# An eight-batch adaLN attention and FFN kernel: TensorE's fillers deepened, the FFN weight's coding spread over GpSimd and ScalarE, ScalarE's first three exponentials moved ahead

## The chip, the cores and the metric

The kernel runs on one core of one Trainium2 chip. The metric is the device time of one execution in microseconds (us), the median of three runs.

## What is computed

The input x is 8 batches of 512 tokens with 256 channels. Two blocks follow each other; the gates, scales and shifts come from a small condition vector.

```python
mod = (_silu(L0_c) @ L0_wmod).reshape(L0_c.shape[0], 6, 1, -1)
sa, ca, ga, sb, cb, gb = (mod[:, 0], ..., mod[:, 5])
h = _layernorm(x, axis=-1) * (1 + ca) + sa
x = x + ga * _L0_attn_ref(h, Wq, bq, Wk, bk, Wv, bv, Wo, bo)
h = _layernorm(x, axis=-1) * (1 + cb) + sb
x = x + gb * _L0_ffn_ref(h, weight, bias)
```

The attention has 16 heads of 16 channels and a log-sparse mask: row i attends to itself and to i - 1, i - 2, i - 4, ... i - 256 (10 offsets), while masked scores count as 0 in the softmax and not as minus infinity. The FFN is one matrix product with both operands quantised in blocks of 32 (amplitude / 7.5 as the scale, values rounded to a 6-bit grid).

## The kernel before

Five engines run programs written out by hand, and semaphores tie them together. All arithmetic is float32 but for the codes (FP8) and three-way split biases (bf16). The work of a batch is a pipeline over all engines, and the programs overlap several batches:

- **ScalarE** (`act`) gathers sums and squares of the next x (`sums_before`, `squares_before`, lines 1188 and 1197), normalises it (`norm_before`, line 1174), evacuates hT, k, v and the attention, computes the exponentials (`exps`, lines 1425 to 1438), takes x1 and its statistics (`take_x1`, `squares_after`), normalises x1 (`norm_after`, line 1174 too), and codes to FP8 (`quantised`, line 1421).
- **TensorE** (`pe`) transposes, projects q, k and v (`k_rows` 826, `q_rows` 837, `v_rows` 853), sums the products of q and shifted k over each head (`head_sums`, 937 and 951), turns the scores to one token per partition (`scores_by_token`, 963 and 966), turns the attention (`attention_transposes`, 893), and does the output projection (988) and the FFN (1067).
- **VectorE** (`dve`) makes ten q-k products per batch (line 1710 for batch 0, in two halves of ten; line 1721 later), the softmax (`softmax_max`, 1802 and 1806; `softmax_weights`, 1819 to 1827), ten products of weight and v (line 1851), and the block maxima and scalings of the quantisation.
- **GpSimd** (`pool`) adds the ten weight-v products of a batch in nine additions (`add`, line 677), gates the projection weights (626, 639), makes 1/sqrt of variances (649, 658) and modulates the second norm (`modulate`, 375 and 380).
- **SyncE** issues all loads and stores. v is written to DRAM and read back shifted by 1 to 64 rows, seven times a batch.

VectorE's loop over batches b does: softmax maximum and weights of b, then weight-v products of b interleaved with q-k products of b+1. ScalarE's iteration b starts with `exps(b)` and ends with `copy_scores(b+1)`, `seed_q(b+2)` and a norm. For iterations 0 to 4 that norm is `norm_before(b+3)`, which waits for GpSimd's 1/sqrt; `exps(b+1)` stands behind it. GpSimd's iteration b is: modulation of b-2, additions 1 to 6 of b with the weight gate between, `rstd_before` or `rstd_both` for the next norms, additions 7 to 9. A weight-v product may be at most four ahead of the additions (a ring of four buffers). SyncE's load of x(b+3) waits for the norm of b+2, as it overwrites its input.

Before the loop, the program turns the weights and works off batch 0. TensorE opens the q banks with bf16 matmuls of three rows of ones and repeats such matmuls (`keep_busy`, line 752) while it waits for the condition vector and for silu. VectorE makes the statistics of batch 0, evacuates wk and wq, seeds q with its bias, then quantises the FFN weight in six steps (`setup_ffn_weight`, lines 1696 to 1703): block maximum, scale, reciprocal, scaling, coding to FP8 by an addition of `TIE_DOWN`, and scaling back. Then come the q-k products of batch 0 (`first_qk_products`), channel half 1 first, and `setup_rows`, which makes the gates. The quantised FFN weight is turned by TensorE in iteration 1 (`weight_transposes(4)`).

## Time and profile before

| what | before |
|---|---|
| median of 3 runs | 286.92 us (286.64 to 287.34) |
| profiled execution, its own time | 286.72 us |
| its span | 285.0 us |
| VectorE busy | 258.8 us, 91% of the span |
| TensorE matmuls busy | 255.6 us, 90% |
| ScalarE busy | 212.5 us, 75% |
| GpSimd busy | 210.5 us, 74% |
| DMA queue of the kernel | 53.63 MB, 60.1% of 16 engines |

The span runs from the first to the last instruction of the profiled execution; 1.7 us of its own time lie outside it. A row of the timeline gives the start and the length of an instruction (or of several of one kind in a row, with their count), and in brackets how long its engine had stood idle before it and which instruction released it. Each float32 matmul that is not a transpose leaves two records. The starts of two rows that follow each other without a bracket are the cost of the first.

### The profile page before, as it was taken

What the parts mean: (1) busy time and instruction counts of PE and PEld (TensorE: products, weight loads), DVE (VectorE), ACT (ScalarE), POOL (GpSimd) and SP (SyncE); (2) the same over time, 40 slices, a digit from 0 to 9 for tenths busy, and PEclk for the clock granted to TensorE, in tenths of its full rate; (3) what the DMA queues carried; (4) which work ended last, traced back from release to release, by engine and by line L of the source; (5) the groups of instructions that cost most, each with busy time, mean ns of one, the idle gap of its engine ahead of it and who ended that gap; (6) DMA issues with size and microseconds to landing.
All of it is one profiled execution on the core that took longest, in us unless ns stands there. A gap on an engine that the chain in (4) does not pass through costs nothing.

```text
span 285.0 us, 4442 instructions
## 1 busy us (share of the span) xinstructions
PE 255.6 (90%) x1368; PEld 158.8 (56%) x1368; DVE 258.8 (91%) x326; ACT 212.5 (75%) x577; POOL 210.5 (74%) x152
## 2 busy tenths in 40 slices
PE   6999997697978795989999999999999988997885
PEld 1653554175526561666556646664567646794663
DVE  3699799969995999999999999999999999999970
ACT  2386987975697779879898989887776937575752
POOL 7101439895879999999999999999999699845100
PEclk9999999999999999999999999999999999999999
DMA  7743977694784239724993389347943965730005
GB/s 225 193 181 81 340 248 232 230 338 133 240 273 148 73 125 350 251 72 131 295 336 127 129 263 286 135 113 222 333 147 94 279 198 178 230 103 11 0 26 199
DMA packets 54399, 53.91 MB, mean 189 GB/s; under 512 B 4100, under 2 KB 52824, under 8 KB 54376
## 3 DMA queue, kind: packets, MB, share of 16 engines
q1 hardware_dynamic: 54376, 53.63, 60.1%
q8 instruction: 11, 0.18, 0.3%
q14 instruction: 12, 0.10, 0.1%
HBM read 44.90 MB, written 8.72 MB: 188 GB/s over the span
## 4 chain that ended last, share of the span: by engine, by line
DVE 39%; POOL 19%; PE 18%; issue 11%; ACT 11%; DVEq 0%; POOLq 0%; ACTq 0%
POOL pv_buf L677 14%; DVE prod L1721 9%; DVE pv_buf L1851 9%; DVE prod L1851 4%; DVE prod L1710 4%; PE ps L988 3%; PE ps L1067 3%; PE ps L826 2%; ACT dump L1197 2%; PE ps L853 2%; ACT dump L1238 1%; DVE ps L1825 1%; PE ps L837 1%; DVE ps L1827 1%; POOL rstd L658 1%
## 5 line engine op out<-in xcount | busy, mean ns | idle before, releaser
L677 POOL TENSOR_TENSOR pv_buf<-pv_buf 128x1024 f32<-128x1024 f32 (+2 forms) x60 | 132.5, 2209 | 15.0 <-DVE pv_buf L1851 9.8
L1721 DVE TENSOR_TENSOR prod<-ps,kT 128x1024 f32<-128x1024 f32 (+4 forms) x70 | 75.1, 1110 | 0.0
L1851 DVE TENSOR_TENSOR pv_buf<-v_shift,ps 128x1024 f32<-128x1024 f32 x49 | 59.1, 1212 | 0.0
L937 PE MATMUL ps<-prod,sel_sum 128*32 128x512 f32 x256 | 30.8, 598 | 8.5 <-DVE prod L1721 7.8
L853 PE MATMUL ps<-wT,h_cen 128*128 128x256 f32 x128 | 29.9, 379 | 0.0
L826 PE MATMUL ps<-hT,wT 128*128 128x512 f32 x64 | 29.7, 596 | 0.0
L837 PE MATMUL ps<-hT,wT 128*128 128x512 f32 x64 | 29.3, 599 | 0.0
L988 PE MATMUL ps<-wo_g,w_raw 128*128 128x256 f32 x112 | 27.9, 392 | 0.0
L853 PEld LDWEIGHTS ps<-wT,h_cen 128*128 128x128 f32 x128 | 23.9, 190 | 6.4 <-issue 3.8
L988 PEld LDWEIGHTS ps<-wo_g,w_raw 128*128 128x128 f32 x112 | 20.1, 189 | 5.4 <-issue 3.2
L937 PEld LDWEIGHTS ps<-prod,sel_sum 128*32 128x32 f32 x256 | 6.7, 109 | 28.0 <-issue 13.8
L1067 PE MATMUL ps<-wf_g,w_raw 128*128 128x256 f32 x80 | 19.7, 391 | 0.0
L1851 DVE TENSOR_TENSOR pv_buf<-v_base,ps 128x1024 f32<-128x1024 f32 (+2 forms) x21 | 19.4, 950 | 0.2
L1291 ACT ACTIVATE kT<-ps,bias_cols 128x512 f32<-128x512 f32 x16 | 10.9, 686 | 11.6 <-PE ps L826 11.6
L649 POOL TENSOR_TENSOR rstd<-var,minus_half 128x4 f32<-128x4 f32 x4 | 4.1, 1016 | 20.1 <-ACT var L1201 19.3
L1174 ACT ACTIVATE x_norm<-x_in,shift,rstd 128x256 f32<-128x256 f32 x28 | 14.5, 594 | 5.6 <-POOL shift L651 3.2
L837 PEld LDWEIGHTS ps<-hT,wT 128*128 128x128 f32 x64 | 11.7, 190 | 12.4 <-issue 12.4
L826 PEld LDWEIGHTS ps<-hT,wT 128*128 128x128 f32 x64 | 11.6, 190 | 10.5 <-issue 9.0
L1067 PEld LDWEIGHTS ps<-wf_g,w_raw 128*128 128x128 f32 x80 | 14.5, 189 | 3.6 <-issue 2.0
L1174 ACT ACTIVATE x_norm<-x,shift,rstd 128x256 f32<-128x256 f32 x28 | 14.5, 592 | 1.4 <-POOL shift L668 1.4
L380 POOL TENSOR_TENSOR h<-x_norm,rows_mod 128x1024 f32<-128x1024 f32 x6 | 14.2, 2362 | 0.5
L375 POOL TENSOR_TENSOR x_norm<-x_norm,rows_mod 128x1024 f32<-128x1024 f32 x6 | 14.2, 2364 | 0.3 <-ACT x_norm L1174 0.2
(212 smaller groups left out, 550.3 us busy)
## 6 DMA issues: line engine op xcount, KB each, us to landing
v_shift<-v_rows SPq DMA_DIRECT2D x56, 512.0 KB, 5.7
x_in<-in_L_attn_x SPq DMA_DIRECT2D x8, 512.0 KB, 4.4
v_rows<-v_base SPq DMA_DIRECT2D x8, 512.0 KB, 4.1
x_res<-in_L_attn_x SPq DMA_DIRECT2D x8, 512.0 KB, 6.5
out_x<-outb SPq DMA_DIRECT2D x5, 512.0 KB, 5.8
rows_mod<-mod_rows SPq DMA_DIRECT2D x7, 256.0 KB, 3.4
x<-in_L_wmod SPq DMA_DIRECT2D x1, 1024.0 KB, 7.9
row_ga<-mod_rows SPq DMA_DIRECT2D x8, 128.0 KB, 4.9
```

The source lines that it names most:

```text
L375: ops.tensor_tensor(normed[:, t, :], normed[:, t, :], rows[:, 0:1, :].broadcast_to([P, n, D]), ALU.mult).then_inc(scaled, 1)
L380: ops.tensor_tensor(dst[:, t, :], normed[:, t, :], rows[:, 1:2, :].broadcast_to([P, n, D]), ALU.add).then_inc(done, 1)
L677: nc.gpsimd.tensor_tensor(dst, dst, ring(b, n)[:, t:NT, :], ALU.add).then_inc(s_add, 1)
L826: mm = nc.tensor.matmul(ps23[:, j, :], wT[:, 1, k, P * j:P * j + P], hT[:, k, :], start=(k == 1), stop=(k == 0))
L837: mm = nc.tensor.matmul(ps01[:, j, :], wT[:, 0, k, P * j:P * j + P], hT[:, k, :], start=False, stop=(k == NC - 1), skip_group_check=True)
L853: mm = nc.tensor.matmul(ps23[:, k2, col:col + D], h_cen[:, k, P * t:P * t + P], wT[:, 2, k, :], start=(t % 2 == 0 and k == 0), stop=(t % 2 ...
L937: mm = nc.tensor.matmul(ps23[32 * g:32 * g + 32, 1, :], sel_sum[:, which, c, :], prod[:, n, c, :], start=(c == 0 and which == 0), stop=(c ...
L988: mm = nc.tensor.matmul(ps[:, k2, col:col + D], attnT[:, k, P * t:P * t + P], wo_by[b][:, k, :], start=False, stop=(t % 2 == 1 and k == NC ...
L1067: mm = nc.tensor.matmul(ps[:, half_, col:col + D], xdT_by[b][:, k, P * t:P * t + P], wf_by[b][:, k, :], start=False, stop=(t % 2 == 1 and ...
L1174: ins = nc.scalar.activation(dst[:, t, :], src[:, t, :], ACT.Identity, scale=rstd[:, t:t + 1], bias=shift[:, t:t + 1])
L1721: nc.vector.tensor_tensor(prod[:, n, :, o:L], ps01[:, :, o:L], kT[:, b % 2, :, 0:L - o], ALU.mult).then_inc(s_prod, 1)
L1851: nc.vector.tensor_tensor(dst[:, t:NT, :].rearrange("p t (h e) -> p t h e", e=DH), v_n.rearrange("p t (h e) -> p t h e", e=DH), weights, A ...
```

## The change

TensorE: `warm_up(ps, bank, n)` issues n float32 matmuls of the 128x128 identity by itself. Three of them run as soon as the identity exists (`s_const` at 2), ahead of the opening of the q banks; one takes the place of the three `keep_busy` matmuls ahead of the condition's transposes, and four take the place of the four behind them. `keep_busy` remains for one place near the end.

The FFN weight: VectorE keeps the block maximum, scale and reciprocal. GpSimd does the two products with the scale (`scale_ffn_weight`, both between `rstd_before(0)` and `rstd_before(1)`), and ScalarE makes the codes (`ffn_weight_codes`, between `evacuate_k(0, 0)` and `sums_before(1)`). A semaphore `s_wfq` chains the six steps over the three engines.

ScalarE's order: `centre_h(1)` moves from ahead of `exps(0)` to behind it. `norm_before(3)` and `norm_before(4)` move from the ends of iterations 0 and 1 to iterations 1 and 2, behind `exps` and `mean_of_v`. From iteration 2 on the norm stands at the end as before.

```diff
         @block.gpsimd
+            def scale_ffn_weight(src, factor, after):
+                pool.wait_ge(s_wfq, after)
+                nc.gpsimd.tensor_tensor(w_raw[:, 4, :, :].rearrange("p c (g k) -> p (c g) k", k=BLOCK),
+                                        src.rearrange("p (g k) -> p g k", k=BLOCK), over(factor[:, :], BLOCK),
+                                        ALU.mult).then_inc(s_wfq, 1)
...
             rstd_before(0)
+            scale_ffn_weight(w_raw[:, 4, :, :].rearrange("p c k -> p (c k)"), wf_inv, WF_SCALED - 1)
+            scale_ffn_weight(wf_q[:, :], wf_scale, WF_CODES)
             rstd_before(1)
...
         @block.tensor
+            def warm_up(ps, bank, n):
+                for i in range(n):
+                    nc.tensor.matmul(ps[:, bank, 0:P], ident[:, :], ident[:, :], start=True, stop=True)
+
+            pe.wait_ge(s_const, 2)
+            warm_up(ps67, 1, 3)
             pe.wait_ge(s_const, CONST_EARLY)
...
-            keep_busy(ps67, 1, 3)
+            warm_up(ps67, 1, 1)
             pe.wait_ge(s_cond, 16)
...
-            keep_busy(ps67, 1, 4)
+            warm_up(ps67, 1, 4)
...
                 if i == 4:
-                    pe.wait_ge(s_cset, SETUP_WF)
+                    pe.wait_ge(s_wfq, WF_DONE)
                     pe.wait_ge(s_x1, 1)
...
         @block.scalar
+            def ffn_weight_codes():
+                act.wait_ge(s_wfq, WF_SCALED)
+                act.wait_ge(s_const, 3)
+                nc.scalar.activation(wf_q[:, :], w_raw[:, 4, :, :].rearrange("p c k -> p (c k)"), ACT.Identity,
+                                     bias=tie[:, 0:1], saturate=False).then_inc(s_wfq, 1)
...
             evacuate_k(0, 0)
+            ffn_weight_codes()
             sums_before(1)
...
             seed_q(1)
-            centre_h(1)
 
             for b in range(LAST - 1):
                 ahead, norm1 = has(b + 2), has(b + 3)
                 exps(b)
+                if b == 0:
+                    centre_h(1)
                 if has(b - 1):
                     mean_of_v(b - 1)
+                if 0 < b < TAIL - 1:
+                    norm_before(b + 2)
...
                 if has(b + 2):
                     seed_q(b + 2)
-                if has(b + 3):
+                if b >= TAIL - 2 and has(b + 3):
                     norm_before(b + 3)
-                elif has(b - 1):
+                elif b >= TAIL - 2 and has(b - 1):
                     norm_after(b - 1)
...
         @block.vector
-            def setup_ffn_weight():
+            def ffn_weight_scales():
                 dve.wait_ge(s_w_in[4], 16)
...
-                link(nc.vector.tensor_tensor(wf_b, wf_b, over(wf_inv[:, :], BLOCK), ALU.mult))
-                link(nc.vector.tensor_scalar(wf_q[:, :], w_raw[:, 4, :, :].rearrange("p c k -> p (c k)"), TIE_DOWN,
-                                             None, ALU.add, saturate=False))
-                link(nc.vector.tensor_tensor(wf_b, wf_qb, over(wf_scale[:, :], BLOCK), ALU.mult))
```

TAIL is 4 and LAST is 7. Three places show how the programs move.

TensorE at its start, before; `h` is the condition vector, `pv_buf` the weights of the modulation:

```order
L747 MATMUL ps<-ones 128x512 x2
L752 MATMUL ps<-ones 128x512 x3
L758 MATMUL ps<-ident,h 128x8 x2
L752 MATMUL ps<-ones 128x512 x4
L765 MATMUL ps<-pv_buf,siluT 32x128 x8
L782 MATMUL ps<-ident,w_raw 128x128 x4
L791 MATMUL ps<-ident,pv_buf 128x128
```

And with the change:

```order
L757 MATMUL ps<-ident 128x128 x3
L763 MATMUL ps<-ones 128x512 x2
L757 MATMUL ps<-ident 128x128
L774 MATMUL ps<-ident,h 128x8 x2
L757 MATMUL ps<-ident 128x128 x4
L781 MATMUL ps<-pv_buf,siluT 32x128 x8
L798 MATMUL ps<-ident,w_raw 128x128 x4
L807 MATMUL ps<-ident,pv_buf 128x128
```

Seven fillers of three rows became eight of 128 rows and 128 columns, three of them ahead of the first row of before; all that follows keeps its order.

ScalarE from the scores of batch 0 to the evacuation of k of batch 1, before (`hT` is the modulated input, `h_cen` the centred one, `em` and the `score_buf` rows of 2x160 the exponentials):

```order
L1446 ACTIVATE score_buf<-ps 128x512
L1265 ACTIVATE hT,h_sum<-ps,cols 128x512 x2
L1284 ACTIVATE ps<-bias_cols 128x512 x2
L1275 ACTIVATE h_off<-h_sum 128x2
L1278 ACTIVATE h_cen<-hT,h_off 128x512 x2
L1425 ACTIVATE em<-mx 128x64
L1430 ACTIVATE ps<-em 128x4x16
L1433 ACTIVATE ps<-score_buf 128x2x160
L1435 ACTIVATE ps<-score_buf 128x2x160
L1291 ACTIVATE kT<-ps,bias_cols 128x512 x2
```

And with the change:

```order
L1468 ACTIVATE score_buf<-ps 128x512
L1287 ACTIVATE hT,h_sum<-ps,cols 128x512 x2
L1306 ACTIVATE ps<-bias_cols 128x512 x2
L1447 ACTIVATE em<-mx 128x64
L1452 ACTIVATE ps<-em 128x4x16
L1455 ACTIVATE ps<-score_buf 128x2x160
L1457 ACTIVATE ps<-score_buf 128x2x160
L1297 ACTIVATE h_off<-h_sum 128x2
L1300 ACTIVATE h_cen<-hT,h_off 128x512 x2
L1313 ACTIVATE kT<-ps,bias_cols 128x512 x2
```

The two rows of `h_off` and `h_cen` went from ahead of the four exponential rows to behind them.

ScalarE between the scores of batch 1 and the v of batch 2, before (`x_norm<-x_in` is `norm_before(3)`):

```order
L1446 ACTIVATE score_buf<-ps 128x512
L1284 ACTIVATE ps<-bias_cols 128x512 x2
L1174 ACTIVATE x_norm<-x_in,shift,rstd 128x256 x4
L1425 ACTIVATE em<-mx 128x64
L1430 ACTIVATE ps<-em 128x4x16
L1433 ACTIVATE ps<-score_buf 128x2x160
L1435 ACTIVATE ps<-score_buf 128x2x160
L1307 ACTIVATE v_mean<-ps,bias_cols 128x1 x2
L1298 ACTIVATE v_base<-ps 128x512
L1318 ACTIVATE w_raw<-ps,v_mean 128x512 x2
```

And with the change:

```order
L1468 ACTIVATE score_buf<-ps 128x512
L1306 ACTIVATE ps<-bias_cols 128x512 x2
L1447 ACTIVATE em<-mx 128x64
L1452 ACTIVATE ps<-em 128x4x16
L1455 ACTIVATE ps<-score_buf 128x2x160
L1457 ACTIVATE ps<-score_buf 128x2x160
L1329 ACTIVATE v_mean<-ps,bias_cols 128x1 x2
L1196 ACTIVATE x_norm<-x_in,shift,rstd 128x256 x4
L1320 ACTIVATE v_base<-ps 128x512
L1340 ACTIVATE w_raw<-ps,v_mean 128x512 x2
```

The norm of batch 3 now stands behind the exponentials of batch 1 and the mean of v; the same happens to the norm of batch 4 an iteration later, where it comes directly ahead of the second norm of batch 0.

## Rows read from the trace of the kernel before

**Rows 1.** Two stages: window, us, busy PE, PEld, DVE, ACT, POOL; clock, DMA

```profile
0.00:32.11 32.11, 28.87 (x158) 15.67 (x159) 24.54 (x59) 17.78 (x45) 7.14 (x35) 1.00 0.61 188
...
95.07:217.90 122.83, 117.20 (x622) 72.41 (x622) 121.12 (x129) 103.74 (x282) 118.41 (x63) 1.00 0.62 195
```

**Rows 2.** Waits of VectorE (waiting line, releaser: us in total, times, longest)

```profile
DVE ps L1819 <- ACT ps L1433: 5.7, 4, 2.2
```

**Rows 3.** Timeline of VectorE, start (start us, us, line, operation, shapes [idle before])

```profile
14.63 0.69 DVE L1700 TENSOR_TENSOR w_raw<-w_raw,wf_inv 128x512 f32<-128x512 f32 x1
...
16.55 10.98 DVE L1710 TENSOR_TENSOR prod<-ps,kT 128x512 f32<-128x512 f32 x20
```

**Rows 4.** Timeline of TensorE, the first 16 us

```profile
2.36 1.03 PE L747 MATMUL ps<-ones 3*128 3x512 bf16 x2 [2.36 <-POOL siluT L579]
...
4.86 1.86 PE L752 MATMUL ps<-ones 3*128 3x512 bf16 x4
6.89 1.08 PE L765 MATMUL ps<-pv_buf,siluT 128*32 128x128 f32 x16 [0.17 <-DVE siluT L1632]
7.91 1.12 PE L782 MATMUL ps<-ident,w_raw 128*128 128x128 f32 x4
...
9.37 1.97 PE L800 MATMUL ps<-ident,x_norm 128*128 128x128 f32 x8
...
13.96 1.88 PE L837 MATMUL ps<-hT,wT 128*128 128x512 f32 x4
15.68 0.60 PE L782 MATMUL ps<-ident,w_raw 128*128 128x128 f32 x4
```

**Rows 5.** Timeline of ScalarE: first normalisation, first scores, first exponentials

```profile
8.09 1.09 ACT L1181 ACTIVATE x_norm<-x_in,shift,rstd 128x256 f32<-128x256 f32 x2 [2.86 <-POOL shift L651]
...
28.78 0.60 ACT L1444 ACTIVATE score_buf<-ps 128x512 f32<-128x512 f32 x1 [2.40 <-PE ps L937]
...
34.23 0.24 ACT L1425 ACTIVATE em<-mx 128x64 f32<-128x64 f32 x1
```

**Rows 6.** Source of two lines: the FP8 coding and the one FP8 product on GpSimd

```profile
L1421 ACT ACTIVATE q_last<-v_shift,tie x2: 722/722/722, 270.7 to 274.4; 128x512 fp8e4<-128x512 f32 x2
...
L691 POOL TENSOR_TENSOR zq<-q,mx_scale x1: 1919/1919/1919, 226.9 to 226.9; 128x1024 f32<-128x1024 fp8e4 x1
```

**Rows 7.** Groups of TensorE lines, first 13 us (busy us, mean ns | idle before)

```profile
L765 PE MATMUL ps<-pv_buf,siluT 128*32 128x128 f32 x16 | 1.1, 421 | 0.2 <-DVE siluT L1632 0.2
```

**Rows 8.** Timeline of GpSimd, batches 0 to 2

```profile
42.11 9.93 POOL L677 TENSOR_TENSOR pv_buf<-pv_buf 128x1024 f32<-128x1024 f32 x4
...
56.87 2.36 POOL L677 TENSOR_TENSOR pv_buf<-pv_buf 128x1024 f32<-128x1024 f32 x1 [1.27 <-DVE pv_buf L1851]
...
95.07 2.37 POOL L375 TENSOR_TENSOR x_norm<-x_norm,rows_mod 128x1024 f32<-128x1024 f32 x1
```

**Rows 9.** Timeline of ScalarE, the norms near the exponentials of batches 1 and 2

```profile
60.52 2.07 ACT L1174 ACTIVATE x_norm<-x_in,shift,rstd 128x256 f32<-128x256 f32 x4 [1.81 <-POOL shift L651]
...
89.44 2.08 ACT L1174 ACTIVATE x_norm<-x_in,shift,rstd 128x256 f32<-128x256 f32 x4 [1.47 <-POOL shift L660]
```

**Rows 10.** Timeline of VectorE, softmax of batches 0, 1, 2 and 4

```profile
35.21 0.50 DVE L1819 TENSOR_TENSOR ps<-ps,em 128x320 f32<-128x320 f32 x1 [1.29 <-ACT ps L1433]
...
63.49 0.50 DVE L1819 TENSOR_TENSOR ps<-ps,em 128x320 f32<-128x320 f32 x1 [2.19 <-ACT ps L1433]
...
88.53 0.89 DVE L1802 TENSOR_REDUCE mx<-ps 128x64 f32<-128x704 f32 x1 [0.87 <-PE ps L966]
...
92.41 0.50 DVE L1819 TENSOR_TENSOR ps<-ps,em 128x320 f32<-128x320 f32 x1 [2.06 <-ACT ps L1433]
...
148.28 0.89 DVE L1802 TENSOR_REDUCE mx<-ps 128x64 f32<-128x704 f32 x1 [0.64 <-PE ps L966]
```

**Rows 11.** Timeline of TensorE, the turned attention of batches 0 and 2

```profile
66.32 1.06 PE L893 MATMUL ps<-ident,pv_buf 128*128 128x128 f32 x8 [1.75 <-POOL pv_buf L677]
...
123.60 1.06 PE L893 MATMUL ps<-ident,pv_buf 128*128 128x128 f32 x8 [0.95 <-POOL pv_buf L677]
```

More of the change, by code:

```diff
@@ L290, in adaln_block @@
         CONST_ALL = CONST_SUM + NO + 2
-        SETUP_SILU, SETUP_COLS, SETUP_WF, SETUP_MOD, SETUP_ROWS = 3, 5, 11, 12, 16
+        SETUP_SILU, SETUP_COLS, SETUP_MOD, SETUP_ROWS = 3, 5, 6, 10
+        WF_SCALED, WF_CODES, WF_DONE = 4, 5, 6
         PE_COND, PE_MOD, PE_WK, PE_COLS, PE_WQ, PE_WV, PE_ROWS, PE_WO, PE_WF = range(1, 10)
```

21 lines of the change are left out of this document (10 added, 11 removed).

## The prediction

> **What bounds the kernel now.** I read the busy time by stage first, then VectorE's waits, then the timelines where one engine hands over to another.
>
> The first maximum starts at 32.11 us, and the stages show two regimes. Before it VectorE is busy 24.5 of 32.1 us and the other engines have gaps. From 95.07 to 217.90 VectorE is busy 121.1 of 122.8 us, GpSimd 118.4 and TensorE 117.2 [rows 1]. So once the pipeline is full, three engines are saturated, and time won on one of them is worth only what the slowest of the three also wins.
>
> VectorE's waits say where its own slack is: four times it waits for ScalarE's exponentials, 5.7 us in all [rows 2]. Three are large, 1.29, 2.19 and 2.06 us, in the softmax of batches 0, 1 and 2 [rows 10]. In the last two, `norm_before` stands ahead of the exponentials and itself waits 1.81 and 1.47 us for GpSimd [rows 9].
>
> Which engine paces the full pipeline is seen at TensorE's turning of the attention: it waits for GpSimd's last addition in batch 0 (1.75 us) and still in batch 2 (0.95 us, at 123.60) [rows 11]. From there TensorE has no gap worth naming until the maximum of batch 4, where VectorE waits 0.64 us for it [rows 10]. **The end of the kernel is therefore tied to when GpSimd ends its additions of batch 2**, and GpSimd works without a gap from 95.07, where it starts the modulation of batch 0, up to there [rows 1, 8]. A gain survives only if that start moves.
>
> **The start.** VectorE loses the last three quantising steps: 16.55 - 14.63 = 1.92 us ahead of its first q-k product [rows 3]. But that product needs q of channel half 1, whose matmuls end at 13.96 + 1.88 = 15.84 [rows 4]. Without anything else the products start at 15.9, a gain D of **0.65 us**, not 1.92.
>
> The fillers decide the rest. The clock column shows 1.00 in every stage, the first one too [rows 1], yet four transposes take 1.12 us at 7.91 and 0.60 us at 15.68 [rows 4]. So until about 12 us TensorE runs at the lower level, 1.2 GHz, and then at 2.4 GHz. From 2.36 to 6.7 us it had run three-row fillers almost without a gap, and these did not bring the clock up; 128-row work begins at 6.89. With the change such work begins as soon as the identity is made, and densely from 4.9. I take it that the clock comes up before or during the eight transposes of h at 9.37. They then take at most 2 x 0.60 instead of 1.97, and the four of wq behind them 0.6 instead of 1.1. Their inputs end at 8.09 + 1.09 = 9.18 [rows 5], so at best they end at 10.4 instead of 11.3, q ends 1.1 us earlier at 14.75, and the products start at 14.8: D = **1.75**. I take 1.6, near that end, because the deep fillers replace 2 us of filler directly ahead of the work; the clock's moment is not tied to the program, hence not the full end.
>
> A rule of the Trainium skill speaks against the fillers: the page "TensorE: Matmul & The Clock Gate" (Part 1) says that the clock follows how busy the engine is and does not name the depth of the operands, by which the old fillers would do as well, and D would stay 0.65. By its Part 4 transposes do not count like other matmuls; here the clock rose in or right behind a stretch of transposes alone (7.91 to about 12), so the trace does not bear that part out.
>
> Costs of this part. A filler is two records. A record of 512 columns at 2.4 GHz costs 1.88 / 4 = 0.47 at most [rows 4], a quarter of the columns at half the clock 0.24: 0.47 us a filler, four of them 1.9 against the 1.86 of the four old ones: nothing. The other bound is two records of 0.42 us one after the other [rows 7], 0.84 a filler; this is for the range. The product records of line 765 overlapped (16 in 1.08 us), so I take 0.47. The three early fillers (1.4 us from about 1.5) push the opening of the q banks by 0.6 us, and nothing wants that before 10 us. GpSimd's two products (1.24 us, a quarter of 9.93 halved, and half of 1.92 [rows 6, 8]) lie where it idles: it is busy 7.1 us of the first stage, and its last work before them ends at 8.1 [rows 1, 5]. ScalarE's coding is 0.72 us [rows 6]; it ends before the v and norm of the next batch, behind which ScalarE waits 2.4 us for the head sums [rows 5]: nothing on the path. The spill of v and its shifted loads start 0.6 us later; VectorE had no wait for them in the trace, and its first use comes behind the whole softmax. If that cover went, it would be 0.6 us.
>
> Products, head sums, scores, gates and maximum of batch 0 all follow the products: they move by D.
>
> **The exponentials of batch 0.** The maximum takes 0.89 us; the exponentials can start at 33.05 instead of 34.23 [rows 5, 10]. VectorE's wait of 1.29 shrinks to about 0.1: it gains 1.2. ScalarE, which used to centre h while the maximum ran, now waits 0.25 for it and 0.2 for the two subtractions: it comes 0.47 later, and with it the variance of batch 2, GpSimd's 1/sqrt and the first addition (42.11). That addition gains D - 0.47. GpSimd's gap of 1.27 us ahead of addition 6 (56.87 [rows 8]) waits for a VectorE that is now D + 1.2 earlier, so it closes: the additions of batch 0 end D - 0.47 + 1.27 = **D + 0.8** earlier. VectorE's 1.2 are not kept: `copy_scores(1)` sits at the end of the same busy ScalarE, so the maximum of batch 1 comes only D - 0.1 earlier, behind a new wait of 1.3.
>
> **Batch 1.** Its exponentials no longer wait for the norm: 2.19 becomes 0.15, VectorE gains D + 1.9. The next maximum (88.53) depends on another chain: additions of batch 0, attention turned, ScalarE's evacuation and all its work to the scores of batch 2. That gains D + 0.8, so the existing wait of 0.87 grows to 1.9.
>
> **Batch 2.** 2.06 becomes 0.15. But the order on ScalarE is now exponentials, mean of v, norm of batch 4, second norm of batch 0. From the maximum: 1.8 + 0.5 + 0.3 + 2.0 + 2.0 = 6.6 us, and 0.15 to GpSimd: 88.53 + 6.75 = 95.3 where the modulation began at 95.07 [rows 8, 9, 10]. The modulation thus gains (D + 0.8) - 0.2 = **D + 0.6**. Here GpSimd gets a new gap of about 1.3 us: its additions would have allowed D + 1.8. Two orders change without a cost. The norm of batch 3 ended at 60.52 + 2.07 = 62.6 and will end near 64.3 - D, ahead of the turned attention at 66.3 - (D + 0.8) [rows 9, 11]. SyncE's load of x(4) waits for that norm, and behind it in the queue stand the spill and shifts of v(2), whose v ScalarE evacuates only behind the turned attention, as it sums x(4).
>
> **After that** GpSimd is gapless; its 1/sqrt of batch 5 comes D + 0.6 earlier, ScalarE's exponentials of batch 3 still stand behind that norm, and VectorE waits some 1.2 us for them where it had no wait. From there everything moves by D + 0.6.
>
> Sum: 1.6 + 0.6 = 2.2 us. The profiled execution's 286.72 becomes 284.5; the median shown is 0.2 above it, so **284.7 us**. With D from 0.65 to 1.75 the sum is 1.25 to 2.35.
>
> **Rivals.**
> - *The clock does not come up sooner.* For: TensorE was hardly idle before either, so if busy time is what counts, nothing changes. Against: 4.3 us of shallow filler brought no clock [rows 4]. D = 0.65, gain 1.25: 285.7 (285.4 to 286.0).
> - *GpSimd gives it back.* If the gap of 1.27 does not close, because gate or 1/sqrt in front of it come late, and the clock stays: D - 0.47 - 0.2 = 0: 286.9 (286.2 to 287.1). For: ScalarE is busy throughout, and GpSimd's additions hang on its variance. Against: VectorE's product has 0.4 us to spare.
> - *The fillers stand in the way*, the slower side. At 0.84 each, the first three end at 4.1, the q banks and the next at 5.8, the condition's transposes 1.2 late; four more end at 9.4, and the modulation starts 2.5 after its 6.89. With the clock unchanged D = 0.65 - 2.5 = -1.85 and the end moves by +1.25: 288.2. It decides from a delay of 1.25 us, a filler of about 0.67. Against: the overlap of line 765.
>
> **Numbers.** Forecast 0.60, clock unchanged 0.24, given back 0.10, fillers 0.06. What a measurement of this kernel can tell is 0.3%, 0.86 us, so faster means below 286.06: the forecast whole and nearly all of the first rival, 0.83. Same: the second rival and a rest, 0.11. Slower 0.06. The range reaches from 0.9 below the forecast (both gaps smaller than I put them) over the first rival into the second: 283.8 to 286.4.
>
> **What would show it.** Right: first q-k product near 14.9 and eight transposes of h in 1.2 to 1.5 us; waits ahead of the maxima of batches 1 and 2 of 1.3 and 1.9; no gap before addition 6 of batch 0; GpSimd idle about 1.3 ahead of the modulation, which starts near 92.9; a wait for the exponentials of batch 3. Wrong: transposes of 1.97 (first rival), a modulation start past 94.5 (second), line 781 after 7.5 (third), or a turned attention of batch 2 that no longer waits for GpSimd.

## The result, and the profile after

| what | before | after |
|---|---|---|
| median | 286.93 us (286.64 to 287.34, 4 runs) | 290.79 us (289.62 to 291.58, 4 runs) |
| profiled execution, its own time | 286.72 us | 291.35 us |
| its span | 285.0 us | 289.6 us |
| mean granted clock of TensorE in it | 1.00 | 0.953 |

The ratio is 1.013, with a 95% interval of 1.009 to 1.017: the change makes the kernel 3.9 us slower. The prediction was 284.7 us, faster. In the ratios here and below, executions more than 1.5% above the fastest one of their kernel are left out, which matters for one kernel, named there.

The first sign is on the page. This is its clock line, in 40 equal slices of 7.2 us, of the kernel after; that of before has a 9 in all 40:

```profile
PEclk9999997959996999799999999999998999999799
```

The clock goes down in six places, at 44, 58, 88, 119, 222 and 269 us, for 3.4 or 6.8 us each, 27.2 us in all. Here are two of them in windows of the kernel after, each with the stretch just ahead of the fall and the stretch of the fall itself (columns as in [rows 1]: window, length, busy PE, PEld, DVE, ACT, POOL, clock, DMA):

```profile
54.30:57.80 3.50, 1.66 (x17) 1.03 (x9) 2.96 (x4) 3.44 (x13) 3.36 (x3) 0.99 0.86 295
57.80:64.60 6.80, 6.80 (x17) 4.24 (x18) 3.82 (x7) 4.06 (x12) 6.24 (x5) 0.50 1.10 347
85.10:88.50 3.40, 1.21 (x10) 1.13 (x11) 1.56 (x3) 3.37 (x12) 2.48 (x2) 1.00 0.98 290
88.50:95.30 6.80, 6.80 (x18) 4.22 (x17) 4.12 (x7) 4.20 (x12) 6.16 (x5) 0.50 0.07 23
```

Ahead of these two falls TensorE is busy 1.66 of 3.5 us and 1.21 of 3.4 us, ScalarE nearly all the time; then TensorE is busy throughout at half the clock, the lower of its two levels. In the 3.4 us ahead of the falls at 44, 119 and 269 it is busy 0.92, 1.62 and 1.95 us. Ahead of the one at 222 it is busy 3.16 of 3.4 us, sixteen one-column records among them, so idle time is not the whole of it. What stands there, in TensorE's timeline of the kernel after:

```profile
54.85 1.05 PE L896 MATMUL ps<-h_sum,wT 128*128 128x1 f32 x8
57.74 1.12 PE L979 MATMUL ps<-ident,score_buf 128*128 128x128 f32 x4 [1.84 <-ACT score_buf L1468]
58.65 1.78 PE L982 MATMUL ps<-fold,score_buf 128*128 128x48 f32 x8
...
90.63 5.99 PE L853 MATMUL ps<-hT,wT 128*128 128x512 f32 x8
```

And the same place in TensorE's timeline of the kernel before:

```profile
54.26 1.92 PE L937 MATMUL ps<-prod,sel_sum 128*32 128x512 f32 x16 [2.77 <-DVE prod L1721]
56.00 1.04 PE L951 MATMUL ps<-prod,sel_sum 128*32 128x512 f32 x8
56.97 1.05 PE L880 MATMUL ps<-h_sum,wT 128*128 128x1 f32 x8
57.88 0.63 PE L963 MATMUL ps<-ident,score_buf 128*128 128x128 f32 x4
```

Before, TensorE waited 2.77 us for VectorE's products, and the scores' transposes followed the means of v without a wait. Now products and head sums come early, and the wait stands between the one-column means and the transposes of the scores. The transposes take 1.12 us and not 0.63; the eight records of `q_rows` (line 853) take 5.99 us, where eight take 3.67 in the kernel before. The sums of TensorE's waits say it for the whole kernel (waiting line, releaser: us in total, times, longest). Before:

```profile
PE ps L937 <- DVE prod L1721: 7.8, 5, 2.8
PE ps L893 <- POOL pv_buf L677: 4.2, 3, 1.7
```

After:

```profile
PE ps L979 <- ACT score_buf L1468: 6.5, 4, 2.2
PE ps L829 <- ACT x_norm L1196: 2.5, 1, 2.5
```

TensorE does not wait more than before: over the span it is idle 21.9 us (289.6 less 267.7 busy), where it was idle 29.4 (285.0 less 255.6). It waits at another place and for another engine, ScalarE. In ScalarE's timeline of the kernel after:

```profile
56.51 0.20 ACT L1223 ACTIVATE var<-sq 128x4 f32<-128x4 f32 x1
56.62 0.58 ACT L1466 ACTIVATE score_buf<-ps 128x512 f32<-128x512 f32 x1
57.10 0.59 ACT L1468 ACTIVATE score_buf<-ps 128x512 f32<-128x512 f32 x1
```

The copies of the scores have no wait of their own; ScalarE comes to them from the squares of batch 3. The work ahead of them on ScalarE is the same in both orders. The second copy starts at 57.10, as late as in the kernel before (57.11), while the head sums of the batch were done at 54.9 instead of 57.0. Part of that lateness comes from the clock itself: behind the fall at 44 ScalarE waits 1.85 us for the matmuls of k of batch 2, where it waited 0.82 before. The experiments below tell the two parts apart.

VectorE's timeline of the kernel after answers to [rows 3] and [rows 10], start and softmax of batches 0 to 2:

```profile
15.52 1.88 DVE L1729 TENSOR_TENSOR prod<-ps,kT 128x512 f32<-128x512 f32 x3 [1.80 <-PE ps L853]
...
33.09 0.50 DVE L1838 TENSOR_TENSOR ps<-ps,em 128x320 f32<-128x320 f32 x1 [0.21 <-ACT ps L1455]
...
60.46 0.89 DVE L1821 TENSOR_REDUCE mx<-ps 128x64 f32<-128x704 f32 x1 [3.20 <-PE ps L982]
...
62.49 0.50 DVE L1838 TENSOR_TENSOR ps<-ps,em 128x320 f32<-128x320 f32 x1 [0.21 <-ACT ps L1455]
...
90.87 0.89 DVE L1821 TENSOR_REDUCE mx<-ps 128x64 f32<-128x704 f32 x1 [4.21 <-PE ps L982]
...
92.89 0.50 DVE L1838 TENSOR_TENSOR ps<-ps,em 128x320 f32<-128x320 f32 x1 [0.21 <-ACT ps L1455]
```

The three large waits for the exponentials (1.29, 2.19, 2.06) are down to 0.21 each, as the change says. They came back ahead of the maxima, at 3.20 and 4.21. GpSimd's modulation of batch 0 [rows 8] starts at 97.56 where it started at 95.07:

```profile
57.43 1.03 POOL L657 TENSOR_TENSOR rstd<-var,minus_half 128x4 f32<-128x4 f32 x1
...
97.56 2.37 POOL L377 TENSOR_TENSOR x_norm<-x_norm,rows_mod 128x1024 f32<-128x1024 f32 x1 [2.53 <-ACT x_norm L1196]
```

### The profile page after: what moved, and what is told of

It is laid out like the page before. It is cut to its first block, busy times and chain, and to the rows that moved or that the text cites. A ratio compares the mean times of both kernels' runs of the same rounds, so it can differ in the third digit from the quotient of the medians.

```text
span 289.6 us, 4460 instructions
## 1 busy us (share of the span) xinstructions
PE 267.7 (92%) x1377; PEld 169.5 (59%) x1377; DVE 257.1 (89%) x323; ACT 213.7 (74%) x578; POOL 212.5 (73%) x154
## 4 chain that ended last, share of the span: by engine, by line
PE 66%; ACT 19%; DVE 7%; issue 5%; POOL 2%; ACTq 0%; POOLq 0%; DVEq 0%
PE ps L1004 10%; PE ps L853 10%; PE ps L1083 8%; PE ps L842 8%; PE ps L869 7%; ACT dump L1219 4%; DVE prod L1729 4%; ACT dump L1260 4%; PE ps L982 3%; PE ps L953 3%; PE ps L1025 2%; ACT h_cen L1300 2%; PE ps L896 2%; PE ps L979 2%; PE ps L829 2%
## 5 line engine op out<-in xcount | busy, mean ns | idle before, releaser
L853 PE MATMUL ps<-hT,wT 128*128 128x512 f32 x64 | 35.1, 696 | 0.0
L842 PE MATMUL ps<-hT,wT 128*128 128x512 f32 x64 | 30.3, 607 | 0.5 <-ACT hT L1287 0.5
L1004 PE MATMUL ps<-wo_g,w_raw 128*128 128x256 f32 x112 | 29.6, 410 | 0.0
L1004 PEld LDWEIGHTS ps<-wo_g,w_raw 128*128 128x128 f32 x112 | 21.2, 199 | 5.7 <-issue 3.2
L853 PEld LDWEIGHTS ps<-hT,wT 128*128 128x128 f32 x64 | 14.0, 229 | 15.9 <-issue 15.9
L1083 PE MATMUL ps<-wf_g,w_raw 128*128 128x256 f32 x80 | 21.1, 412 | 0.0
L1313 ACT ACTIVATE kT<-ps,bias_cols 128x512 f32<-128x512 f32 x16 | 10.9, 687 | 12.6 <-PE ps L842 12.6
L842 PEld LDWEIGHTS ps<-hT,wT 128*128 128x128 f32 x64 | 12.0, 197 | 11.0 <-issue 10.3
L1083 PEld LDWEIGHTS ps<-wf_g,w_raw 128*128 128x128 f32 x80 | 15.5, 204 | 4.2 <-issue 2.0
L1821 DVE TENSOR_REDUCE mx<-ps 128x64 f32<-128x704 f32 x8 | 7.1, 890 | 11.0 <-PE ps L982 11.0
L1320 ACT ACTIVATE v_base<-ps 128x512 f32<-128x512 f32 x16 | 9.4, 594 | 9.9 <-PE ps L869 9.4
L1239 ACT ACTIVATE x<-ps 128x256 f32<-128x256 f32 x28 | 10.4, 380 | 7.2 <-PE ps L1004 7.2
```

What stands on the lines that cost most here:

```text
L842: mm = nc.tensor.matmul(ps23[:, j, :], wT[:, 1, k, P * j:P * j + P], hT[:, k, :], start=(k == 1), stop=(k == 0))
L853: mm = nc.tensor.matmul(ps01[:, j, :], wT[:, 0, k, P * j:P * j + P], hT[:, k, :], start=False, stop=(k == NC - 1), skip_group_check=True)
L1004: mm = nc.tensor.matmul(ps[:, k2, col:col + D], attnT[:, k, P * t:P * t + P], wo_by[b][:, k, :], start=False, stop=(t % 2 == 1 and k == NC ...
L1083: mm = nc.tensor.matmul(ps[:, half_, col:col + D], xdT_by[b][:, k, P * t:P * t + P], wf_by[b][:, k, :], start=False, stop=(t % 2 == 1 and ...
```

## The experiments

Each ratio is to the kernel before on the same chip, with its 95% interval; medians of the kernel before were 286.63 to 286.93 us.

**The two halves of the change alone.** The first kernel (e1_fill_weight) has the fillers and the FFN weight's new places, with ScalarE's order as before; the second (e2_order_only) is the kernel before with the new order alone.

```diff
 # e1_fill_weight, against the kernel after
+            centre_h(1)
             for b in range(LAST - 1):
...
-                if b == 0:
-                    centre_h(1)
...
-                if 0 < b < TAIL - 1:
-                    norm_before(b + 2)
...
-                if b >= TAIL - 2 and has(b + 3):
+                if has(b + 3):
                     norm_before(b + 3)
-                elif b >= TAIL - 2 and has(b - 1):
+                elif has(b - 1):
                     norm_after(b - 1)
```

> The change without its ScalarE order: deep fillers and the FFN weight over three engines, but centre_h(1) and both norms where they were before. Theory A (the new ScalarE order moves TensorE's wait to a place between the one-column v_means and the narrow score transposes, and there the clock falls): granted clock 1.0 throughout, first product near 15.5, and the start's gain of 1.0 kept: 285.9 us (285.4 to 286.5). Theory B (the early rise that the deep fillers bring is itself the cause; the clock then falls at waits that were there before too): mean clock 0.98 or less and 288 us or more.

Measured: 286.94 us (286.01 to 288.21, 10 runs), ratio 1.001 (0.998 to 1.003). Both theories miss: the clock was not 1.0 but 0.964 to 0.988, and the time lies between their ranges. In its profile the clock fell at 44.7, behind a wait of 2.07 us ahead of the transposes of h of batch 2, which the kernel before has too (2.07), and at 218.8.

> The kernel before with only ScalarE's order changed (centre_h(1) behind exps(0), the norms of batches 3 and 4 behind exps and mean_of_v). Theory A: TensorE waits 1.5 to 2.5 us ahead of the score transposes of batches 1 to 3, the clock falls there, mean clock 0.95 to 0.98, 288.5 to 291.5 us. Theory B: clock 1.0, and the time is that of before or a little less, 286.0 to 287.0. Theory C (no clock at all; the new gap of GpSimd ahead of the modulation costs the time): clock 1.0 and over 288.

Measured: 290.91 us (288.42 to 291.40, 4 runs), ratio 1.013 (1.008 to 1.017). The order alone is the whole loss, so a theory that puts it down to fillers or weight falls. Its waits are those of the kernel after, and so are its falls, at 44, 58, 89, 119, 222 and 270 us. TensorE's timeline and two windows of this kernel:

```profile
43.82 1.57 PE L813 MATMUL ps<-ident,x_norm 128*128 128x128 f32 x8 [2.49 <-ACT x_norm L1174]
...
54.97 1.05 PE L880 MATMUL ps<-h_sum,wT 128*128 128x1 f32 x8
57.90 1.05 PE L963 MATMUL ps<-ident,score_buf 128*128 128x128 f32 x4 [1.88 <-ACT score_buf L1446]
```

```profile
54.30:57.80 3.50, 1.72 (x16) 0.97 (x8) 3.08 (x4) 3.42 (x13) 3.36 (x3) 1.00 1.05 341
57.80:64.60 6.80, 6.70 (x17) 4.24 (x18) 3.73 (x7) 4.12 (x13) 6.35 (x5) 0.52 1.06 335
```

Fillers and weight alone gave nothing in the median, although the first product in its profile came at 15.83, 0.72 us sooner than before; its ten executions ran at clocks of 0.964 to 0.988, so part of the gain may have been lost to falls of the clock as well. This run doesn't settle it.

**Filling the new waits.** If the clock is the cause, filler in the same waits, at no other change, must bring the time back and more. This is the kernel after (here e3_keep_warm), with nine identity matmuls ahead of the transposes of h of batch 2 and eight between the means of v and the scores of batches 1 to 3:

```diff
+                if b == 0:
+                    pe.wait_ge(s_d, 1)
+                    warm_up(ps67, 0, 9)
                 if ahead:
                     h_transposes(b + 2, 1)
...
                 v_means(b)
+                if b < 3:
+                    warm_up(ps67, 0, 8)
                 scores_by_token(b + 1)
```

> The whole change, with deep identity matmuls also in three kinds of wait: 9 ahead of the transposes of h(2) (it waits for s_d(0) first, long given), and 8 between v_means(b) and scores_by_token(b + 1) for b = 0, 1, 2. Theory A: the clock stays up through batches 0 to 3, mean clock 0.985 or more, and what was forecast comes back but for the start: 284.9 to 286.5 us. Theory B: the clock falls elsewhere just as often, mean 0.97 or less, over 288.5. Theory C: clock up but still over 288.

Measured: 286.68 us (285.70 to 286.91, 10 runs), ratio 0.998 (0.996 to 1.001): 4.1 us less than the kernel after (and 4.2 less than the order alone, which ran on the same chip), for matmuls whose results nobody reads. The clock is as theory A has it, 0.988 to 0.994; the median lies 0.2 us above its range. TensorE, ScalarE and VectorE in its timeline, and the windows that answer to those above:

```profile
54.95 2.03 PE L757 MATMUL ps<-ident 128*128 128x128 f32 x16
56.81 0.60 PE L979 MATMUL ps<-ident,score_buf 128*128 128x128 f32 x4
...
54.96 0.59 ACT L1473 ACTIVATE score_buf<-ps 128x512 f32<-128x512 f32 x1
...
86.30 0.89 DVE L1826 TENSOR_REDUCE mx<-ps 128x64 f32<-128x704 f32 x1 [1.83 <-PE ps L982]
```

```profile
54.00:57.40 3.40, 3.40 (x34) 3.37 (x31) 2.45 (x3) 2.52 (x7) 3.26 (x3) 1.00 1.09 356
57.40:60.80 3.40, 3.40 (x16) 1.97 (x15) 2.28 (x5) 1.55 (x7) 3.18 (x4) 1.00 1.09 345
```

The maxima of batches 0 to 3 in the kernel after come 0.82, 2.18, 4.57 and 5.15 us later than here (31.07, 60.46, 90.87 and 120.36 us against 30.25, 58.28, 86.30 and 115.21). So most of the loss arises in batches 1 and 2, around the falls at 44, 58 and 88.

The fillers have a price of their own. The second copy of the scores ends at 54.96 + 0.59 = 55.55, and their transposes start only behind the filler, at 56.81; in batches 2 and 3 they start 0.4 and 1.5 us behind the copy's end. Shorter fillers weren't tried, and neither was it tried which of the four fillers is needed.

With the clock up, the steps of the prediction can be read with the fillers as the only disturbance (in the next section). One fall was left in the profiled execution, in the tail, behind the three fillers of three rows that the change had kept, and sixteen records of the FFN took 5.25 us for the 3.72 of before. In this kernel's timeline:

```profile
262.31 0.81 PE L768 MATMUL ps<-ones 3*128 3x512 bf16 x3
263.55 0.51 PE L1053 MATMUL ps<-bias_ffn,ones 3*128 3x512 bf16 x2 [0.43 <-ACT w_raw L1392]
263.99 5.25 PE L1083 MATMUL ps<-wf_g,w_raw 128*128 128x256 f32 x16
```

The profiled execution was the fastest, 285.70 us. The other nine ran at clocks of 0.988, so with about twice as long at half the clock, and took 286.49 to 286.91; where their clock fell was not seen.

**Busy or deep?** The same kernel with its new fillers as bf16 matmuls of three rows, about as long (e6_shallow_loop):

```diff
-                    warm_up(ps67, 0, 9)
+                    keep_busy(ps67, 0, 9)
...
-                    warm_up(ps67, 0, 8)
+                    keep_busy(ps67, 0, 8)
```

> e3_keep_warm with the fillers of the loop made of three-row bf16 matmuls of 512 columns, as long and as many. If what holds the clock up is the depth of the operands (theory A): it falls at the same places as in the change, mean clock 0.95 to 0.97, 289.5 to 291.5 us. If it is only that TensorE is busy (the rule by busy time): clock as in e3, 286.0 to 287.0.

Measured: 291.42 us (288.70 to 291.85, 4 runs), ratio 1.013 (1.008 to 1.018): all of the gain is gone, as theory A has it. Its timeline and windows:

```profile
55.52 2.38 PE L768 MATMUL ps<-ones 3*128 3x512 bf16 x8
57.83 1.11 PE L979 MATMUL ps<-ident,score_buf 128*128 128x128 f32 x4
```

```profile
53.40:56.80 3.40, 3.40 (x26) 1.68 (x20) 3.40 (x4) 3.30 (x14) 3.26 (x2) 1.00 0.78 270
56.80:63.60 6.80, 6.80 (x19) 4.11 (x18) 2.92 (x7) 3.51 (x11) 6.44 (x6) 0.50 1.09 341
```

TensorE is busy 3.40 of 3.40 us ahead of the fall, as the profile counts it, and the clock falls all the same. By Part 1 of "TensorE: Matmul & The Clock Gate" in the Trainium skill, the clock goes by how busy the engine is; these rows do not agree. What this pair of kernels changes is the depth and type of the filler's operands (128 rows float32 against 3 rows bf16), and with them the number of records and of weight loads (31 loads, busy 3.37 us, in e3's first window against 20, busy 1.68 us, in this one's). Which of these counts wasn't separated.

**Which of the moves.** Three kernels split the order:

```diff
 # e4_centre_back, against the kernel after
+            centre_h(1)
             for b in range(LAST - 1):
...
-                if b == 0:
-                    centre_h(1)
 # e7_centre_only, against the kernel before
-            centre_h(1)
             for b in range(LAST - 1):
...
                 exps(b)
+                if b == 0:
+                    centre_h(1)
 # e8_norms_only, against the kernel before
+                if 0 < b < TAIL - 1:
+                    norm_before(b + 2)
...
-                if has(b + 3):
+                if b >= TAIL - 2 and has(b + 3):
                     norm_before(b + 3)
-                elif has(b - 1):
+                elif b >= TAIL - 2 and has(b - 1):
                     norm_after(b - 1)
```

> The whole change but centre_h(1) back ahead of exps(0). Theory A: the wait ahead of the transposes of h(2) is back at 2.1 us (it was 2.5) and the one ahead of the scores of batch 1 shrinks below 1 us, so no fall of the clock before 60 us; those ahead of the scores of batches 2 and 3 stay, so the mean clock is 0.97 to 0.99 and the time 287.0 to 289.5. Theory B: the clock falls as in the change, 290 to 291.5.

Measured: 287.14 us (286.93 to 289.51, 10 runs), ratio 1.002 (0.999 to 1.005), in theory A's range. But the profile does not follow that theory: the clock fell at 43.4, where none was expected before 60 us, and then only at 121.9. The scores of batch 1 waited 0.34 us and those of batch 2 2.19, and there the clock stayed up:

```profile
85.74 0.66 PE L979 MATMUL ps<-ident,score_buf 128*128 128x128 f32 x4 [2.19 <-ACT score_buf L1468]
```

Seven of the ten executions had clocks of 0.963 to 0.976, and six of these took 287.00 to 287.34 us, hardly more than the three at 0.988 (286.93 to 287.10).

> The kernel before with centre_h(1) behind exps(0) and nothing else. Theory A: ScalarE comes 0.47 later, the wait ahead of the transposes of h(2) grows from 2.1 to 2.5 and a wait of about 1.8 appears ahead of the scores of batch 1; the clock falls at both: mean clock 0.96 to 0.98 and 288 to 290 us. Rival (it takes the moved norms to open the waits): 286.3 to 287.2, clock 0.985 or more.

Measured: 286.99, 288.03, 288.74 and 291.09 us, ratio 1.006 (1.002 to 1.010), with six more of ten left out at 291.56 to 292.67 and clocks of 0.953 to 0.959. The median of all ten is 291.71, so the ratio understates what this move does. Of the ten only the fastest has a profile. There TensorE waited 2.48 us ahead of the transposes of h of batch 2, as in the change, but the clock stayed up until 87.5 us (it fell at 87.5, 111 and 265):

```profile
44.76 1.14 PE L813 MATMUL ps<-ident,x_norm 128*128 128x128 f32 x8 [2.48 <-ACT x_norm L1174]
...
57.47 0.66 PE L963 MATMUL ps<-ident,score_buf 128*128 128x128 f32 x4 [0.50 <-ACT score_buf L1446]
```

The wait ahead of the scores of batch 1 was 0.50 us and not the expected 1.8. Up to these scores this kernel's programs are those of e2_order_only, whose wait was 1.88. Counted from the maximum of batch 0 (32.13 us here, 31.19 there), the head sums end at the same moment in both, 23.8 us, but the second copy starts at 24.7 us here and at 26.1 there, where the clock fell at 44. In e3_keep_warm, whose clock stayed up too, it is 24.7 again, and 26.0 in the kernel after. **So 1.4 of the 1.88 us of the wait at 58 are themselves the work of the fall at 44**: one fall makes the wait behind which the next one comes.

> The kernel before with the two norms behind the exponentials and centre_h(1) in its old place. Theory A: no wait ahead of the scores of batch 1, waits near 2 ahead of those of batch 2 (and a fall there), mean clock 0.97 to 0.99, 286.8 to 288.5 us. Rival (each move costs half): 288.5 to 289.5.

Measured: 289.60 us (289.35 to 290.31, 5 runs), ratio 1.010 (1.006 to 1.013). That is above theory A's range and 0.1 us above the rival's. The scores of batches 1 to 3 waited 0.53, 2.13 and 1.38 us, and the clock fell at 45.0, 86.0 and 116.7, so the wait and the fall at batch 2 are as theory A has them:

```profile
86.49 1.11 PE L963 MATMUL ps<-ident,score_buf 128*128 128x128 f32 x4 [2.13 <-ACT score_buf L1446]
```

Each move alone costs, against the kernel before: the norms 2.7 us, the centring 0.1 to 4.2 us in the four executions counted and 4.7 to 5.8 in the six others. The parts don't add: with fillers and weight in place the norms' move cost hardly anything (287.14). The two waits of 2.19 and 2.13 us at the same scores, one without a fall and one with, show that such a wait makes a fall possible and not certain.

**The tail.** The kernel with the filled waits, and deep filler in the tail in place of and ahead of the three shallow ones; then the same with five matmuls that add the identity times zero to a bank that is in use (no bank was free there), in a wait of 1.29 us:

```diff
 # e5_keep_tail
+            pe.wait_ge(s_d, B)
+            warm_up(ps23, 1, 4)
             xd_transposes(LAST - 2)
-            keep_busy(ps23, 0, 3)
+            warm_up(ps23, 0, 4)
...
 # e9_zero_tail, in addition
             xd_transposes(LAST - 1)
+            pe.wait_ge(s_x1, LAST)
+            for i in range(5):
+                nc.tensor.matmul(ps67[:, 0, 0:P], ident[:, :], siluT[:, 0, B:B + 1].broadcast_to([P, P]),
+                                 start=False, stop=False, skip_group_check=True)
             ffn(LAST - 1, 0)
```

> The fillers of e3_keep_warm, and in the tail too: the three three-row fillers behind the turned xd of batch 5 become four deep ones, and four more stand ahead of those transposes, where TensorE waits 1.1 us for VectorE. Theory A (the time of the change is lost to falls of the clock; in e3 one fall at 263.7 us and others in most runs ate what was left): mean clock 0.994 or more in most runs, median 284.6 to 285.8 us. Rival: the tail does not feel TensorE's clock, or the clock falls elsewhere: 286.3 to 287 as e3.

Measured: 286.39 us (284.67 to 287.46, 12 runs), ratio 0.998 (0.996 to 1.000). That is above theory A's range and in the rival's: one execution of twelve ran at a clock of 1.00, at 284.67. The sixteen records of line 1083 took 3.72 us again, but in the profiled execution the clock fell one step later, at 270.8, behind this wait:

```profile
270.42 0.39 PE L1053 MATMUL ps<-bias_ffn,ones 3*128 3x512 bf16 x2 [1.29 <-ACT kT L1394]
270.74 3.68 PE L1083 MATMUL ps<-wT,kT 128*128 128x256 f32 x8
```

> e5_keep_tail, and five deep matmuls of the identity with a column of zeros, which add 0 to the x1 of batch 6, in TensorE's wait of 1.3 us behind the transposes of batch 6's xd (in e5 the clock fell right behind that wait, at 270.8 us, and the run took 286.4 where the one at full clock took 284.7). Theory A: with that wait filled most runs keep the clock, 0.998 or more, median 284.6 to 285.3 us. Rival (zeros do not hold the clock, or another wait of the tail takes over): 286.0 to 286.6 as e5.

Measured: 285.85 us (284.84 to 287.53, 12 runs), ratio 0.996 (0.994 to 0.998): **1.1 us (0.4%) less than the kernel before**, and the lowest median of this study. It lies between the ranges of theory A and of the rival. Most executions did not keep the clock: one of twelve ran at 1.00, eleven at 0.992 to 0.994. Against e5_keep_tail, on another chip, the two ratios' intervals overlap. The tail, in its timeline:

```profile
270.57 1.28 PE L1180 MATMUL ps<-siluT,ident 128*128 128x128 f32 x10
272.02 0.39 PE L1053 MATMUL ps<-bias_ffn,ones 3*128 3x512 bf16 x2 [0.17 <-ACT kT L1398]
272.34 1.99 PE L1083 MATMUL ps<-wT,kT 128*128 128x256 f32 x8
```

Eight records take 1.99 us here and took 3.68 at the same place in e5_keep_tail.

**The other two parts, with the clock held.** From this best kernel, the start's fillers were made shallow again, and the FFN weight's six steps put back on VectorE.

```diff
 # e10_shallow_start
-            pe.wait_ge(s_const, 2)
-            warm_up(ps67, 1, 3)
...
-            warm_up(ps67, 1, 1)
+            keep_busy(ps67, 1, 3)
...
-            warm_up(ps67, 1, 4)
+            keep_busy(ps67, 1, 4)
 # e11_weight_back
-            scale_ffn_weight(w_raw[:, 4, :, :].rearrange("p c k -> p (c k)"), wf_inv, WF_SCALED - 1)
-            scale_ffn_weight(wf_q[:, :], wf_scale, WF_CODES)
...
-            ffn_weight_codes()
...
-            ffn_weight_scales()
+            setup_ffn_weight()
```

> e9_zero_tail with the fillers of the start as they were before (3 and 4 bf16 matmuls of three rows). What the deep ones are worth at the start: if they bring the clock up about 2 us sooner on average, the first q-k product starts near 15.9 instead of 14.8 and the median is 0.7 to 1.2 us above e9. If depth is nothing there: within 0.3 us of e9.

Measured: 286.33 us (285.77 to 287.29, 12 runs), ratio 0.997 (0.994 to 1.000). At a clock of 1.00 its six executions took 285.77 to 286.14, where the two kernels with deep filler had 284.67 and 284.84, one execution each: the deep filler is worth 0.5 us in the median, between the two expected ranges and not clear of the spread, and about 1 at the full clock. The six executions at 0.993 to 0.994 (median 286.91) and the eleven of e9_zero_tail at 0.992 to 0.994 (median 285.95) also differ by about 1. The median hides it because six of twelve kept the clock here and one of twelve there; why is not known. In the profile the clock rose only at 13.7 us, and the first product came at 16.76. The deep fillers also start earlier, at 1.6 us, and this part of their effect wasn't told apart from depth.

> e9_zero_tail with all six steps of the FFN weight on VectorE again. The three steps are 1.9 us ahead of the first product, of which VectorE would otherwise wait about 1.6 for q when the clock comes up late and less when early: the first product near 15.7, the median 0.7 to 1.2 us above e9. If the weight's place is nothing: within 0.3 us of e9.

Measured: 286.01 us (285.20 to 286.55, 12 runs), ratio 0.997 (0.995 to 0.998). At a clock of 1.00 it took 285.20 to 285.27 in three executions. The weight's new places are worth 0.2 us in the median, which the spread doesn't tell from nothing (the second of the two expectations), and 0.4 to 0.6 at the full clock, against the same two single executions.

**One fall in the full pipeline.** In the profiled execution of the best kernel the clock fell at 218.9 us, behind sixteen one-column records in a row. The last kernel (e12_split_means) parts them, and ScalarE reads both means later:

```diff
             v_means(LAST - 1)
-            v_means(LAST)
             project(LAST - 2)
+            v_means(LAST)
...
-            mean_of_v(LAST - 1)
-            mean_of_v(LAST)
             take_x1(LAST - 2, 0)
...
             seed_ffn_half(LAST - 4, 1)
+            mean_of_v(LAST - 1)
+            mean_of_v(LAST)
```

> The kernel of e9_zero_tail with one thing moved: the eight one-column matmuls of the mean of v of the last batch go from right behind those of the batch before it to behind the output projection of batch 5, and ScalarE reads both means behind x1 of batch 5. In the profiled e9_zero_tail the only fall of the clock before the end stood at 218.9 us, right behind sixteen one-column matmuls in a row (215.47, 1.92 us, 0.26 idle before them), with TensorE never idle longer. Theory A (one-column matmuls count as little as three-row ones, so a stretch of them is a gap to the clock): the fall at 219 goes; executions at a clock of 1.00 become common, at 284.7 to 284.9 us, and the median goes from 285.85 to about 285.1 (284.8 to 285.5), a ratio to the kernel before of 0.993 to 0.995. Rival B (the falls that are left come at moments that the program does not set): clocks stay at 0.992 to 0.994 in nearly all executions and the median at 285.6 to 286.1. Rival C (the two means are wanted earlier than the trace shows, and the move delays the work of batch 6): slower by 0.3 us or more than e9_zero_tail at the same clock, 285.1 at 1.00.

Measured: 286.64 us (284.71 to 287.03, 12 runs), ratio 0.997 (0.995 to 1.000). The clock fell at 218.9 again, in a stretch that now has eight one-column records and a wait of 0.72 us, as its timeline shows:

```profile
215.48 1.02 PE L896 MATMUL ps<-h_sum,wT 128*128 128x1 f32 x8 [0.24 <-ACT v_base L1331]
217.22 0.37 PE L994 MATMUL ps<-bias_att,ones 3*128 3x512 bf16 x1 [0.72 <-ACT ps L1357]
```

Theory A fails as stated: one execution of twelve ran at 1.00, at 284.71. At that clock rival C fails too. At 0.994 it doesn't: the eleven executions took 286.12 to 287.03 us (median 286.67), where seven of e9_zero_tail took 285.39 to 287.53 (median 285.43), and no run shows why. Rival B had the clocks right, but the time lies above its range. The move changed two things at once, means and wait, so what one-column matmuls count for stays open.

## Why the prediction was wrong

**The step that failed** is the passage on the exponentials of batch 0. It says of ScalarE that "it comes 0.47 later", and then: "`copy_scores(1)` sits at the end of the same busy ScalarE, so the maximum of batch 1 comes only D - 0.1 earlier, behind a new wait of 1.3". It saw that ScalarE becomes the last to arrive, and priced it as a wait of GpSimd and of VectorE. The same lateness is a wait of TensorE, at two places: ahead of the transposes of h of batch 2, where it grows from 2.07 to 2.48 us, and ahead of the transposes of the scores, next to one-column matmuls. The sum puts what such waits do to TensorE's clock at nothing. The same holds for its batches 1 and 2, where the moved norms open a wait of 2.1 to 2.2 us ahead of the scores of batch 2, and under "after that" TensorE is not mentioned at all.

What the runs put in its place: with the waits filled 286.68, with the same waits filled by shallow matmuls 291.42, with them open 290.79. The missing term is 4.1 us in the median. Of the 6.1 us between forecast and result this leaves 2.0; no median closes them, only the single executions at a clock of 1.00 of kernels with filler in the tail too. In the profiled execution 27.2 us ran at half the clock. At full clock TensorE's work of that time would have taken some 13.6 us less; that the kernel lost only 4.1 shows that most of this did not stand on the path that decides the end.

The prediction even had the pieces: it argued at the start that shallow work does not raise the clock, and did not ask where the change would leave stretches of that kind.

**Point by point**, in the kernel after and, with the clock up but with the fillers' own length in it, in e3_keep_warm's profile:

| step | forecast | after | waits filled |
|---|---|---|---|
| D, start of the first product | 1.6 | 1.03 | 1.86 |
| eight transposes of h, us | 1.2 to 1.5 | 1.24 | 1.09 |
| wait for exponentials of batch 0 | 0.1 | 0.21 | 0.21 |
| wait ahead of the maximum of batch 1 | 1.3 | 3.20 | 1.83 |
| wait ahead of the maximum of batch 2 | 1.9 | 4.21 | 1.83 |
| gap ahead of GpSimd's addition 6, batch 0 | none | none | none |
| GpSimd's gap, start of the modulation | 1.3, 92.9 | 2.53, 97.56 | 1.08, 92.99 |
| wait for the exponentials of batch 3 | 1.2 | none | 0.44 |
| turned attention of batch 2 waits for GpSimd | yes | no, 126.59 | yes, 121.49 [1.09] |

- *The start.* Right in kind. The clock was up at 10.0 us, and the transposes took 1.24 us instead of 1.97 [rows 4]. Over the eight profiles with both parts in place the first product came at 14.69 to 15.87, so D was 0.68 to 1.86, since the moment of the rise differs between executions; the assumed 1.6 is near the upper end. Luck enters on both sides: e2_order_only, with the shallow fillers, had its first product at 15.62, a D of 0.93, because its clock rose at 10.2.
- *Fillers.* The four take 2.08 us, about 0.52 each, and `modulation` of the condition started at 7.16 against 6.89 [rows 4]: a delay of 0.27, where that rival needed 1.25. It falls.
- *Batches 0 to 2.* With the clock held, D + 0.6 says a modulation at 95.07 - 2.46 = 92.61; it came at 92.99, which is D + 0.2. The other five profiles with deep fillers in the loop and a clock that stays up through these batches (e5, e9, e10, e11, e12) show D + 0.2 as well. Part of the missing 0.4 may be the fillers themselves: VectorE waited 1.83 us for the maximum of batch 1 with them and 0.66 in e7_centre_only without, where the forecast had 1.3. For the end of the kernel D + 0.6 says 286.72 - 2.46 = 284.3 for that profiled execution; it took 285.70 with the fall in the tail, which made 5.25 us of 3.72 and so accounts for about 1.5. At the full clock e5, e9 and e12 took 284.67, 284.84 and 284.71. That this meets the forecast of 284.7 is in part luck: these kernels have fillers that the forecast did not know, and D in these executions wasn't seen. The one profiled execution at a clock of 1.00 that has the change's order, that of e11, took 285.27 us with a D of 1.32: a gain of 1.45, which is D + 0.1 and not D + 0.6.
- *"TensorE has no gap worth naming"* was read from the trace of before, and held for it. The change is what made gaps. A statement of that kind has to be made again for the new order.
- *The rivals.* None was the right one. The slower side was given to fillers in the way, at 0.06; the mechanism that decided, a clock that is lost again in the loop, was not among them.

## What to carry to other kernels

When a wait is taken from one engine, find the engine that arrives last next, and list everyone who waits for it; on TensorE a new wait of about 2 us between thin matmuls can cost more than the wait itself, because the clock may fall behind it for several us of dense work, and the slower work opens the next wait. Where such a wait can't be avoided, fill it with matmuls of full depth into a free bank, and look at the clock line of the profile before anything else. Size the filler by the wait at the full clock: here the waits read off a profile with falls were up to 1.4 us too long. Busy time alone does not say that a filler works.

## What the runs showed of the hardware

- TensorE busy 3.40 of 3.40 us with three-row bf16 matmuls among others, and the clock fell to half behind it; with 128-row float32 matmuls at the same place it stayed up.
- A matmul of the identity with zeros, ten records in 1.28 us, stood in the one tail wait where the clock had fallen before, and in this profile it did not fall. That zeros hold the clock as other data do is suggested by this one profile against one, and not shown: eleven of this kernel's twelve executions still ran at 0.992 to 0.994.
- Seven profiled kernels leave the wait of 2.07 to 2.49 us ahead of the transposes of h of batch 2 open. Behind it the clock fell in five (the kernel after, e1, e2, e4, e8), whose clock had first risen at 9.3 to 10.9 us, and not in two (the kernel before, e7), where it had risen at 12.1 and 12.4. Whether the moment of the rise decides it isn't settled by these.
- A fall need not cost time. In one set of 29 executions of the kernel before, the eleven at a clock of 0.986 to 0.988 took 286.39 to 287.20 us, and the eight at 1.00 took 286.31 to 286.84. The six at 0.976 or less took 287.59 to 290.21.
- Under a program that does not change, the clock differs: the kernel before ran at means of 0.965 to 1.00 and 286.3 to 290.2 us in the same 29 executions, the best kernel at 0.992 to 1.00. With one fall or little more (a clock of 0.992 to 0.994) the best kernel took 285.39 to 287.53 us, against 284.84 at 1.00: 0.5 to 2.7 us. Small gains here are seen only among executions of the same clock.
- The first rise came between 7.7 and 13.7 us, over the profiled executions: 7.7 to 10.7 us in the nine with deep filler at the start (from 1.6 us on), 10.2 to 13.7 in the five with shallow (from 2.4 us on). The two ranges overlap, so the deep filler brings it sooner in most executions, not in each.
